# When and in what order the seven right operands of a stage are made, in a one-core fp32 transformer block

## The chip, the cores and the metric

The kernel runs on one NeuronCore of a Trainium2 chip. The metric is the device time of one execution in microseconds (us), from start to end. The profiled execution's span, from its first to its last instruction, is a little shorter than its device time.

## What is computed

The input x has 2048 tokens of 512 features. All of it is float32.

```python
x = x + attn_block(layernorm(x))       # 512x512 matrices Wk, Wv, Wr, Wo, then Wkey/Wval, Wcr
    # inside: kk = mix(h) @ Wkey.T     # 512 -> 2048
    #         kv = silu(kk) @ Wval.T   # 2048 -> 512, gated by sigmoid(... @ Wcr.T)
gate, up = split(layernorm(x) @ w_gate_up.T)   # 512 -> 2 * 2048
x = x + (silu(gate) * up) @ w_down.T           # 2048 -> 512
```

The change touches only the way in which the right-hand operands of two products are prepared: `mix(h) @ Wkey.T` and `layernorm(x) @ w_gate_up.T`.

## The kernel before, in words

Every float32 matrix product is made of three TensorE passes: an operand is split into a high part (a copy rounded to `fp32r`) and a low part (the operand minus its high part), and high x high, high x low and low x high are added in PSUM. In the order of the code, ScalarE makes high parts, VectorE or GpSimd makes low parts by a subtraction.

After the attention part (up to about 250 us of the span) the rest runs as 48 **units**, `unit(u)` on each engine, in **four stages** that begin at units 0, 8, 16 and 32 (`FIRST`). Units 0 to 15 are key units (Wkey), 16 to 47 gate units (w_gate_up). Stages 0 and 1 are the key units of the first and second pair of token blocks; stages 2 and 3 the gate units of the two pairs. A unit takes its left operand from weights (`left`) and its right one from tokens (`combo`). It computes a 2x2 block product by the seven products of a Strassen-Winograd scheme, each of 6 matmuls (`product`, L489 to L499). The right operands of the seven are called B11, T3, T2, B21, T1, T4 and B22, and here each product goes by the name of its right operand. TensorE's order in a unit is: B11, T3, output tiles (slot 0), T2, B21, tiles (slot 1), T1, tiles (slot 2), T4, B22, tiles (slot 3). An output tile is 6 matmuls (L485 to L487) of an earlier unit's result with the down projection; a key unit has two per slot, a gate unit one (unit 17 has tiles in slots 0 and 2 alone).

All units of a stage share one set of right operands. There is one set of places for them, `combo[:, c]`. So at each stage start all seven have to be made anew, each after the last product of the old stage that reads its place (`used[c]`, L366), and before the first product of the new stage that reads it: in the first unit of a stage TensorE waits for `combo_lo` to reach a count which goes by the operand's place in `MADE_ORDER` (L492). Per operand c the steps are

- the sum or difference: `right_sums` (L1211, makes T3 and T1, 4 VectorE operations), `make_t2` (L1241, 2, overwrites B11's tokens), `make_t4` (L1248, 2, overwrites B21's tokens and needs T2);
- `combo_hi_of` (L851): two ScalarE copies of 128x512, after `used[c]`;
- `combo_lo_of` (L1235): two VectorE subtractions of 128x512, each after its copy.

Every engine runs its queue strictly in the order in which the code lists it. Other work in the same queues that the change's order bears on, per unit:

- VectorE: `accumulate` (L1255, frees the PSUM bank of an output tile, which TensorE takes again four tiles later), `seed` (L1308, after T2; TensorE's T1 product waits for it), `sum_v` (L1317, after T1; TensorE's B22 product waits for it, L693), `sums(u + 1)` (L1200, four 128x256 sums for the next unit's left operand in stages 0 and 2), `gate` (L1321, twice in a gate unit; TensorE's T3 product of the next unit waits for both, L679).
- ScalarE: the copies of X (L916, TensorE's T2 waits for it) and of V (L922), `unit_left_hi` (L826, its second part after `sums`), `unit_right_hi`, `key_tile` and `gate_tile` (the SiLUs; TensorE's next unit waits for them).
- GpSimd: `unit_left_lo` (L1477), `unit_right_lo`, `inner_lo_tile`: subtractions of SBUF tiles.

`after` is the new stage in the last unit before it (units 7, 15 and 31). `SUMS_UNIT` names the units in which `right_sums` runs for stages 1, 2 and 3: 4, 14 and 30.

Of the kernel before, what the change touches and what calls it, by code (L numbers as in the profile page):

```python
# [87 lines left out]
A11, A12, A22, S1, S2, S3, S4 = range(SEVEN)  # L88
B11, B21, B22, T4, T1, T2, T3 = range(SEVEN)

MADE_ORDER = (B11, T3, T2, B21, T1, B22, T4)


def stage_of(u):
    return max(n for n in range(STAGE_COUNT) if FIRST[n] <= u)


def stage_start(u):
    return u in FIRST
# [107 lines left out]
def build(nc, x, wts, wide, tall, vectors, identity, out):  # L207
# [3 lines left out]
    with ExitStack() as ctx:  # L211
# [515 lines left out]
        def _(act):  # L727
# [98 lines left out]
            def unit_left_hi(u, part):  # L826

                if part == 0:
                    act.wait_ge(quart_loaded, 16 * (fresh_until(u) + 1))
                    if u >= 2:  # L830
                        act.wait_ge(p3, u - 1)
                    else:
                        act.wait_ge(cr_psum, SUBS * (BLOCKS if u else 2))
                    if u - 2 in FRESH:
                        act.wait_ge(left_kept[u % 2], 16 * same_parity(FRESH, u - 2))
                    act.activation(left[u % 2][:, 0, 0:3, :], quart[:, 1:4, :], ACT.Copy).then_inc(left_hi, 1)
                else:
                    act.wait_ge(sums_done, 4 * (fresh_until(u) + 1))
                    act.activation(left[u % 2][:, 0, 3:7, :], quart[:, 4:8, :], ACT.Copy).then_inc(left_hi, 1)  # L839
# [11 lines left out]
            def combo_hi_of(stage, c):  # L851
                if stage:
                    act.wait_ge(used[c], FIRST[stage])
                else:
                    act.wait_ge(o_psum, SUBS * BLOCKS)
                if c in (T1, T2, T3, T4):
                    act.wait_ge(t_made, 8 * stage + 2 * ((T3, T1, T2, T4).index(c) + 1))
                elif stage == 0:
                    act.wait_ge(ck_made, 2 * KT)
                elif stage == 1:  # L860
                    act.wait_ge(raw_back[0], 16)
                    act.wait_ge(raw_back[1], 16)
                else:
                    act.wait_ge(t3_kept, 2 * SUBS * (stage - 1))
                for k in range(2):
                    act.activation(combo[:, c, k, 0, :], combined(stage, c, k), ACT.Copy).then_inc(combo_hi, 1)
# [6 lines left out]
            def key_tile(u, n, source):  # L873
                tile = 4 * u + n
                b, i = KEY_TILES[n]
                if u:
                    act.wait_ge(inner_lo, tile - RING + 1)
                else:
                    act.wait_ge(op_lo, OPERANDS)
                act.activation(made_at(tile), source[:], ACT.Silu).then_inc(silu_done, 1)  # L880
                if u == 0 and n == 0:
                    act.wait_ge(combo_lo, 2 * SEVEN)
                if u == 1 and n == 0:
                    act.wait_ge(raw_kept[0], 16)
                    act.wait_ge(raw_kept[1], 16)
                act.wait_ge(silu_done, tile + 1)
                inner_hi_tile(tile, 2 * u + b, i)
# [20 lines left out]
            def unit(u):  # L908

                after = stage_of(u + 1) if u + 1 < UNITS and stage_start(u + 1) else None  # L910
                act.wait_ge(p1, u + 1)
                if u:
                    act.wait_ge(silu_done, silu_by(u - 1, 3 if is_key(u - 1) else 1))
                else:
                    act.wait_ge(sr_ready, SUBS * BLOCKS)
                act.activation(Y[:], X[:], ACT.Copy).then_inc(x_copied, 1)  # L916
                if after is not None:
                    combo_hi_of(after, B11)
                act.wait_ge(p7, u + 1)
                if u:  # L920
                    act.wait_ge(v_summed, u)
                act.activation(seventh[:], V[:], ACT.Copy).then_inc(seventh_copied, 1)  # L922
                if u > KEYS:
                    gated_hi(u - 1)
                for j in range(BLOCKS):
                    if u == NORM3_UNIT[j]:
                        norm3(j)
                if stage_start(u) and u:
                    combo_hi_of(stage_of(u), B22)
                if after is not None:  # L930
                    combo_hi_of(after, T3)
                if u + 1 in FRESH:
                    unit_left_hi(u + 1, 0)
                if is_key(u) and u:
                    unit_right_hi(u)
                spread = u in FIRST[1:]
                if u + 1 in FRESH and not spread:
                    unit_left_hi(u + 1, 1)
                act.wait_ge(p2, u + 1)
                if is_key(u):  # L940
                    key_tile(u, 0, X)
                    if u == 0:
                        unit_right_hi(u)
                else:
                    gate_tile(u, 0, X)
                if stage_start(u) and u:
                    combo_hi_of(stage_of(u), T4)
                if not is_key(u):
                    unit_right_hi(u)
                if u + 1 in FRESH and spread:  # L950
                    unit_left_hi(u + 1, 1)
                if after is not None:
                    combo_hi_of(after, T2)
                    combo_hi_of(after, B21)
                    combo_hi_of(after, T1)
                if is_key(u):
                    act.wait_ge(p4, u + 1)
                    key_tile(u, 1, Z)
                    act.wait_ge(v_summed, u + 1)
                    key_tile(u, 2, V)  # L960
                act.wait_ge(p3, u + 1)
                if is_key(u):
                    key_tile(u, 3, Y)
                else:
                    gate_tile(u, 1, Y)
# [49 lines left out]
            unit_left_hi(0, 1)  # L1015
            combo_hi_of(0, B21)
            combo_hi_of(0, T1)
            combo_hi_of(0, B22)
            combo_hi_of(0, T4)
            channel_receptance(3)  # L1020
            act.activation(table[:], minus_half[:, 0, 0:1], ACT.Silu).then_inc(table_loaded, 1)
            for u in range(UNITS):
# [4 lines left out]
        def _(dve):  # L1027
# [207 lines left out]
            def combo_lo_of(stage, c):  # L1235
                for k in range(2):
                    dve.wait_ge(combo_hi, 2 * (SEVEN * stage + MADE_ORDER.index(c)) + k + 1)
                    dve.tensor_tensor(combo[:, c, k, 1, :], combined(stage, c, k), combo[:, c, k, 0, :].bitcast(F32),  # L1238
                                      ALU.subtract).then_inc(combo_lo, 1)
# [91 lines left out]
            def unit(u):  # L1331

                after = stage_of(u + 1) if u + 1 < UNITS and stage_start(u + 1) else None
                def some(slot):
                    for n in tiles_in(u, slot):
                        accumulate(n)

                if stage_start(u) and u:
                    combo_lo_of(stage_of(u), T1)
                some(0)  # L1340
                seed(u)
                if stage_start(u) and u:
                    make_t4(stage_of(u))
                    combo_lo_of(stage_of(u), B22)
                if after is not None:
                    combo_lo_of(after, B11)
                if u + 1 in FRESH and not stage_start(u):
                    sums(u + 1)
                if is_key(u):
                    last_norm(u, 0)  # L1350
                some(1)
                if stage_start(u) and u:
                    combo_lo_of(stage_of(u), T4)
                sum_v(u)
                if u == 0:
                    first_chunk_right_lo()
                if stage_start(u) and u and u + 1 in FRESH:
                    sums(u + 1)
                if after is not None:
                    make_t2(after)  # L1360
                    combo_lo_of(after, T3)
                some(2)
                if not is_key(u):
                    gate(u, 0)
                    gate(u, 1)
                if after is not None:
                    combo_lo_of(after, T2)
                some(3)
                if u in SUMS_UNIT:
                    right_sums(SUMS_UNIT.index(u))  # L1370
                last_norm(u, 1)
                if after is not None:
                    combo_lo_of(after, B21)

            first_norm1()
            last_of_r_lo()
# [53 lines left out]
            combo_lo_of(0, B21)  # L1430
            make_t4(0)
            combo_lo_of(0, T1)
            combo_lo_of(0, B22)
            combo_lo_of(0, T4)
            sums(1)
            for u in range(UNITS):
                unit(u)
# [175 lines left out]
```

## Time and profile before

| what | value |
|---|---|
| device time, median of 3 runs | 1074.23 us (1073.85 to 1074.23) |
| device time of the profiled execution | 1074.51 us |
| its span | 1072.7 us |
| TensorE busy | 1057.1 us, 99% |
| VectorE, ScalarE, GpSimd busy | 59%, 45%, 50% |
| granted TensorE clock, mean | 0.998 |

Engines in rows: PE is TensorE's matmul, DVE is VectorE, ACT is ScalarE, POOL is GpSimd. In a row of a timeline stand the start (us from the span's start), the time it took, the engine, the line, the operation, the tiles written and read, the shapes and the number of instructions merged into the row; a bracket tells how long the engine was idle before it and what released it. A matmul's recorded 0.39 us overlaps the next one's, so idle time on TensorE is read from starts: here and below a "group" is six matmuls, those of one product or one output tile.

### The profile page before, as it was taken

To read this page: it belongs to the slowest core of one execution; us is meant where nothing else is said; L and a number is where in the kernel's file an instruction comes from. 1 tells how busy PE (TensorE), PEld (TensorE's weight loads), DVE (VectorE), ACT (ScalarE), POOL (GpSimd) and SP (SyncE) were. 2 spreads that over 40 slices of the span, in tenths; PEclk is the share of its full clock that TensorE was granted. 3 is DMA by queue.
4 is the path that set the end of the run, shared out by engine and by line. 5 is a ranking of instruction groups with operands and counts; after the bars stand their busy time and mean duration, and the time that the engine had idled before them with its cause. 6 is when DMAs were issued, how large, how long until landed. Compare 5 with 4: busy or idle time off the path is not lost.

```text
span 1072.7 us, 13182 instructions
## 1 busy us (share of the span) xinstructions
PE 1057.1 (99%) x4748; PEld 873.8 (81%) x4748; DVE 632.5 (59%) x1104; ACT 484.2 (45%) x808; POOL 540.2 (50%) x453
## 2 busy tenths in 40 slices
PE   7999999999999999999999999999999999999998
PEld 6888888788888888888887888888887888888887
DVE  7888656786545545555459567676658333333334
ACT  6866676766444454333355433434354222222221
POOL 6686373735755545445345655555553333333322
PEclk9999999999999999999999999999999999999999
DMA  8002042267653345742412757564554464344422
GB/s 317 1 1 40 1 99 83 95 202 282 231 182 122 128 157 158 225 128 89 157 50 99 243 208 238 207 188 153 197 183 150 149 234 155 106 141 152 153 79 79
DMA packets 45234, 157.19 MB, mean 147 GB/s; under 512 B 4080, under 2 KB 4208, under 8 KB 40560
## 3 DMA queue, kind: packets, MB, share of 16 engines
q1 hardware_dynamic: 29712, 108.02, 28.8%
q0 software_dynamic: 15168, 48.24, 15.0%
q8 instruction: 38, 0.62, 0.2%
q14 instruction: 28, 0.23, 0.1%
q10 hardware_dynamic: 288, 0.09, 0.0%
HBM read 97.60 MB, written 58.72 MB: 146 GB/s over the span
## 4 chain that ended last, share of the span: by engine, by line
PE 87%; DVE 7%; POOL 2%; ACT 1%; DMA 1%; issue 1%; SPq 0%; ACTq 0%; DVEq 0%
PE bank L485 15%; PE bank L486 15%; PE bank L487 15%; PE bank L496 13%; PE bank L497 13%; PE bank L498 13%; DVE combo L1238 2%; DMA quart<-wide 1%; POOL operand L1459 1%; PE bank L555 1%; PE bank L653 1%; DVE resid L1264 1%; POOL weights L1447 0%; POOL weights L1459 0%; DVE raw L1245 0%
## 5 line engine op out<-in xcount | busy, mean ns | idle before, releaser
L1264 DVE TENSOR_TENSOR resid<-bank,resid 128x512 f32<-128x512 f32 x240 | 165.1, 690 | 239.8 <-PE bank L487 238.5
L1503 POOL TENSOR_TENSOR inner<-made,inner 128x512 fp32r<-128x512 f32 x128 | 166.8, 1326 | 200.5 <-ACT inner L871 200.5
L496 PE MATMUL bank<-combo,left 128*128 128x512 f32 x672 | 262.7, 391 | 4.7 <-DVE combo L1238 3.1
L498 PE MATMUL bank<-combo,left 128*128 128x512 f32 x672 | 261.5, 389 | 0.0
L497 PE MATMUL bank<-combo,left 128*128 128x512 f32 x672 | 261.5, 389 | 0.0
L485 PE MATMUL bank<-right,inner 128*128 128x512 f32 x512 | 199.2, 389 | 0.0
L486 PE MATMUL bank<-right,inner 128*128 128x512 f32 x512 | 199.2, 389 | 0.0
L487 PE MATMUL bank<-right,inner 128*128 128x512 f32 x512 | 199.2, 389 | 0.0
L1481 POOL TENSOR_TENSOR left<-quart,left 128x512 fp32r<-128x512 f32 x96 | 115.4, 1225 | 91.3 <-ACT left L839 46.8
L496 PEld LDWEIGHTS bank<-combo,left 128*128 128x128 f32 x672 | 126.1, 188 | 34.1 <-DVE combo L1238 4.0
L498 PEld LDWEIGHTS bank<-combo,left 128*128 128x128 f32 x672 | 126.1, 188 | 26.2
L497 PEld LDWEIGHTS bank<-combo,left 128*128 128x128 f32 x672 | 126.2, 188 | 25.7
L485 PEld LDWEIGHTS bank<-right,inner 128*128 128x128 f32 x512 | 96.1, 188 | 20.1
L487 PEld LDWEIGHTS bank<-right,inner 128*128 128x128 f32 x512 | 96.1, 188 | 20.0
L486 PEld LDWEIGHTS bank<-right,inner 128*128 128x128 f32 x512 | 96.1, 188 | 19.9
L1498 POOL TENSOR_TENSOR right<-tall_staged,right 128x512 fp32r<-128x512 f32 x62 | 80.8, 1312 | 59.2 <-ACT right L849 59.2
L892 ACT ACTIVATE made<-bank 128x512 f32<-128x512 f32 x64 | 38.1, 595 | 154.0 <-PE bank L498 154.0
L1459 POOL TENSOR_TENSOR operand<-made,operand 128x512 fp32r<-128x512 f32 x64 | 83.6, 1406 | 35.1 <-ACT operand L736 35.1
L1329 DVE TENSOR_TENSOR made<-bank,made 128x512 f32<-128x512 f32 x64 | 44.2, 691 | 60.4 <-ACT made L892 39.1
L871 ACT ACTIVATE inner<-made 128x512 fp32r<-128x512 f32 x128 | 77.2, 628 | 2.5 <-DVE made L1329 0.2
L880 ACT ACTIVATE made<-bank 128x512 f32<-128x512 f32 x64 | 37.6, 587 | 85.7 <-PE bank L498 85.7
L485 PE MATMUL bank<-operand,weights 128*128 128x512 f32 x176 | 69.5, 395 | 1.8 <-ACT held L763 1.8
(133 smaller groups left out, 1457.7 us busy)
## 6 DMA issues: line engine op xcount, KB each, us to landing
kept_left<-left SPq DMA_DIRECT2D x24, 1792.0 KB, 8.1
left<-kept_left POOLq DMA_DIRECT2D x24, 1024.0 KB, 6.9
left<-kept_left POOLq DMA_DIRECT2D x24, 768.0 KB, 5.0
tall_staged<-tall SPq DMA_DIRECT2D x64, 256.0 KB, 2.9
quart<-wide SPq DMA_DIRECT2D x24, 512.0 KB, 4.2
raw<-kept SPq DMA_DIRECT2D x32, 256.0 KB, 6.3
landed<-wts SPq DMA_DIRECT2D x20, 256.0 KB, 6.3
resid<-x POOLq DMA_DIRECT2D x4, 1024.0 KB, 9.2
```

Of the source, the lines that this page charges most:

```text
L485: pe.matmul(acc, left(0), right(0), start=first, stop=False)
L486: pe.matmul(acc, left(0), right(1), start=False, stop=False)
L487: return pe.matmul(acc, left(1), right(0), start=False, stop=last)
L496: pe.matmul(acc[:], hi, combo[:, c, k, 0, :], start=fresh and k == 0, stop=False, skip_group_check=True)
L497: pe.matmul(acc[:], hi, combo[:, c, k, 1, :], start=False, stop=False, skip_group_check=True)
L498: mm = pe.matmul(acc[:], lo, combo[:, c, k, 0, :], start=False, stop=k == 1, skip_group_check=True)
L871: act.activation(inner[:, h % 4, i, 0, :], made_at(n), ACT.Copy).then_inc(inner_hi, 1)
L1264: dve.tensor_tensor(tile, A[s][:], tile, ALU.add).then_inc(added, 1)
L1459: pool.tensor_tensor(place(kind, b, k, 1), made[:, (n + k) % RING, :], place(kind, b, k, 0).bitcast(F32), ALU.subtract).then_inc(op_lo, 1)
L1481: lo = pool.tensor_tensor(left[u % 2][:, 1, a[0]:a[0] + n, :], quart[:, a[0] + 1:a[0] + 1 + n, :], left[u % 2][:, 0, a[0]:a[0] + n, :].bit ...
L1498: pool.tensor_tensor(right[:, g % 2, i, 1, :], tall_staged[i][:], right[:, g % 2, i, 0, :].bitcast(F32), ALU.subtract).then_inc(right_lo, 1)
L1503: pool.tensor_tensor(inner[:, h % 4, i, 1, :], made_at(n), inner[:, h % 4, i, 0, :].bitcast(F32), ALU.subtract).then_inc(inner_lo, 1)
```

## The change

Three things, by the diff:

- In the last unit of a stage (7, 15, 31) ScalarE copies T2 just before that unit's first SiLU, and T4 before the last one, where T4 was copied in the first unit of the new stage. VectorE makes B11's low part first of all, T2 (`make_t2`) before `seed`, T3's low part behind `seed`, T2's low part before `sum_v`, B21's low part and T4 (`make_t4`) before the tiles of slot 2, and T1's low part before the tiles of slot 3. In the first unit of the stage T4's and B22's low parts are left.
- `right_sums` stands in units 4, 14 and 30 behind `sum_v`, no more behind the tiles of slot 3.
- T4 and B22 change places in `MADE_ORDER`, in ScalarE's and VectorE's queues ahead of unit 0, and in the first unit of a stage. TensorE's own order is unchanged.

No operation is added or taken away.

```diff
@@ -88,7 +88,7 @@
 A11, A12, A22, S1, S2, S3, S4 = range(SEVEN)
 B11, B21, B22, T4, T1, T2, T3 = range(SEVEN)
 
-MADE_ORDER = (B11, T3, T2, B21, T1, B22, T4)
+MADE_ORDER = (B11, T3, T2, B21, T1, T4, B22)
 
 
 def stage_of(u):
@@ -936,6 +936,8 @@
                 spread = u in FIRST[1:]
                 if u + 1 in FRESH and not spread:
                     unit_left_hi(u + 1, 1)
+                if after is not None:
+                    combo_hi_of(after, T2)
                 act.wait_ge(p2, u + 1)
                 if is_key(u):
                     key_tile(u, 0, X)
@@ -943,14 +945,11 @@
                         unit_right_hi(u)
                 else:
                     gate_tile(u, 0, X)
-                if stage_start(u) and u:
-                    combo_hi_of(stage_of(u), T4)
                 if not is_key(u):
                     unit_right_hi(u)
                 if u + 1 in FRESH and spread:
                     unit_left_hi(u + 1, 1)
                 if after is not None:
-                    combo_hi_of(after, T2)
                     combo_hi_of(after, B21)
                     combo_hi_of(after, T1)
                 if is_key(u):
@@ -958,6 +957,8 @@
                     key_tile(u, 1, Z)
                     act.wait_ge(v_summed, u + 1)
                     key_tile(u, 2, V)
+                if after is not None:
+                    combo_hi_of(after, T4)
                 act.wait_ge(p3, u + 1)
                 if is_key(u):
                     key_tile(u, 3, Y)
@@ -1015,8 +1016,8 @@
             unit_left_hi(0, 1)
             combo_hi_of(0, B21)
             combo_hi_of(0, T1)
+            combo_hi_of(0, T4)
             combo_hi_of(0, B22)
-            combo_hi_of(0, T4)
             channel_receptance(3)
             act.activation(table[:], minus_half[:, 0, 0:1], ACT.Silu).then_inc(table_loaded, 1)
             for u in range(UNITS):
@@ -1335,42 +1336,43 @@
                     for n in tiles_in(u, slot):
                         accumulate(n)
 
-                if stage_start(u) and u:
-                    combo_lo_of(stage_of(u), T1)
-                some(0)
-                seed(u)
-                if stage_start(u) and u:
-                    make_t4(stage_of(u))
-                    combo_lo_of(stage_of(u), B22)
                 if after is not None:
                     combo_lo_of(after, B11)
+                some(0)
+                if after is not None:
+                    make_t2(after)
+                seed(u)
+                if after is not None:
+                    combo_lo_of(after, T3)
+                if stage_start(u) and u:
+                    combo_lo_of(stage_of(u), T4)
                 if u + 1 in FRESH and not stage_start(u):
                     sums(u + 1)
                 if is_key(u):
                     last_norm(u, 0)
                 some(1)
                 if stage_start(u) and u:
-                    combo_lo_of(stage_of(u), T4)
+                    combo_lo_of(stage_of(u), B22)
+                if after is not None:
+                    combo_lo_of(after, T2)
                 sum_v(u)
                 if u == 0:
                     first_chunk_right_lo()
                 if stage_start(u) and u and u + 1 in FRESH:
                     sums(u + 1)
+                if u in SUMS_UNIT:
+                    right_sums(SUMS_UNIT.index(u))
                 if after is not None:
-                    make_t2(after)
-                    combo_lo_of(after, T3)
+                    combo_lo_of(after, B21)
+                    make_t4(after)
                 some(2)
                 if not is_key(u):
                     gate(u, 0)
                     gate(u, 1)
                 if after is not None:
-                    combo_lo_of(after, T2)
+                    combo_lo_of(after, T1)
                 some(3)
-                if u in SUMS_UNIT:
-                    right_sums(SUMS_UNIT.index(u))
                 last_norm(u, 1)
-                if after is not None:
-                    combo_lo_of(after, B21)
 
             first_norm1()
             last_of_r_lo()
@@ -1430,8 +1432,8 @@
             combo_lo_of(0, B21)
             make_t4(0)
             combo_lo_of(0, T1)
+            combo_lo_of(0, T4)
             combo_lo_of(0, B22)
-            combo_lo_of(0, T4)
             sums(1)
             for u in range(UNITS):
                 unit(u)
```

## Rows read from the trace of the kernel before

**Rows 1.** The page, engines: busy us, share of the span, instructions.
```profile
PE 1057.1 (99%) x4748; PEld 873.8 (81%) x4748; DVE 632.5 (59%) x1104; ACT 484.2 (45%) x808; POOL 540.2 (50%) x453
```
**Rows 2.** Waits of PE: who for whom, us in total, times, longest.
```profile
PE bank L496 <- DVE combo L1238: 3.1, 2, 2.0
```
**Rows 3.** Timeline of PE at the starts of stages 2 and 3.
```profile
571.91 0.47 PE L496 MATMUL bank<-combo,left 128*128 128x512 f32 x1 [0.33 <-issue]
...
579.71 0.50 PE L496 MATMUL bank<-combo,left 128*128 128x512 f32 x1 [0.75 <-DVE bank L1315]
...
583.91 0.50 PE L496 MATMUL bank<-combo,left 128*128 128x512 f32 x1 [1.19 <-DVE combo L1238]
...
589.69 0.50 PE L496 MATMUL bank<-combo,left 128*128 128x512 f32 x1
...
824.60 0.39 PE L486 MATMUL bank<-right,inner 128*128 128x512 f32 x1
824.83 0.39 PE L487 MATMUL bank<-right,inner 128*128 128x512 f32 x1
827.17 0.50 PE L496 MATMUL bank<-combo,left 128*128 128x512 f32 x1 [1.95 <-DVE combo L1238]
```
**Rows 4.** Timelines of DVE and POOL: the same operations together and apart.
```profile
563.85 3.00 DVE L1245 TENSOR_TENSOR raw<-raw 128x512 f32<-128x512 f32 x2
...
563.30 2.99 POOL L1481 TENSOR_TENSOR left<-quart,left 128x512 fp32r<-128x512 f32 x2 [3.19 <-ACT left L839]
...
809.51 1.29 DVE L1245 TENSOR_TENSOR raw<-raw 128x512 f32<-128x512 f32 x2
...
587.09 2.54 POOL L1481 TENSOR_TENSOR left<-quart,left 128x512 fp32r<-128x512 f32 x2 [8.04 <-ACT left L839]
...
572.68 5.78 DVE L1238 TENSOR_TENSOR combo<-raw,combo 128x512 fp32r<-128x512 f32 x4
```
**Rows 5.** Timelines of PE, DVE and POOL in unit 30 and early in 31.
```profile
792.38 0.39 PE L496 MATMUL bank<-combo,left 128*128 128x512 f32 x1
...
793.94 0.70 DVE L1319 TENSOR_TENSOR bank<-bank,e 128x512 f32<-128x512 f32 x1 [0.67 <-PE bank L498]
...
798.65 0.69 DVE L1329 TENSOR_TENSOR made<-bank,made 128x512 f32<-128x512 f32 x1 [1.23 <-ACT made L892]
...
799.99 1.29 DVE L1223 TENSOR_TENSOR extra<-raw 128x512 f32<-128x512 f32 x2
...
792.71 4.50 POOL L1481 TENSOR_TENSOR left<-quart,left 128x512 fp32r<-128x512 f32 x4 [3.62 <-ACT left L836]
797.16 1.29 POOL L1498 TENSOR_TENSOR right<-tall_staged,right 128x512 fp32r<-128x512 f32 x1
...
800.54 0.39 PE L496 MATMUL bank<-combo,left 128*128 128x512 f32 x1
```
**Rows 6.** Timelines of DVE, ACT, POOL and PE in unit 15.
```profile
555.19 1.98 POOL L1481 TENSOR_TENSOR left<-quart,left 128x512 fp32r<-128x512 f32 x2 [4.28 <-ACT left L836]
557.13 2.98 POOL L1498 TENSOR_TENSOR right<-tall_staged,right 128x512 fp32r<-128x512 f32 x2
...
561.71 0.42 DVE L1209 TENSOR_TENSOR quart<-quart 128x256 f32<-128x256 f32 x1
...
563.25 0.69 DVE L1319 TENSOR_TENSOR bank<-bank,e 128x512 f32<-128x512 f32 x1
...
562.16 1.06 ACT L839 ACTIVATE left<-quart 128x1024 fp32r<-128x1024 f32 x1 [6.01 <-DVE quart L1209]
...
565.98 0.39 PE L496 MATMUL bank<-combo,left 128*128 128x512 f32 x1
```
**Rows 7.** Timelines of ACT and PE ahead of unit 0 and in it.
```profile
247.51 1.15 ACT L866 ACTIVATE combo<-held 128x512 fp32r<-128x512 f32 x2 [2.65 <-DVE held L1252]
248.57 1.55 ACT L824 ACTIVATE raw<-bank 128x512 f32<-128x512 f32 x3
...
250.95 1.28 ACT L1021 ACT_TABLE_LOAD   x1
...
252.99 0.50 PE L496 MATMUL bank<-combo,left 128*128 128x512 f32 x1
...
276.70 0.50 PE L496 MATMUL bank<-combo,left 128*128 128x512 f32 x1 [0.25 <-DVE bank L1319]
```

## The prediction, made before the change was run

> **What bounds the kernel now.** I read the page's busy shares first: TensorE is busy 99% of the span [rows 1], so nothing elsewhere can pay unless it removes a hole on TensorE. The list of TensorE's waits then says what the holes are: the largest item in the units is the low parts of the right operands, two waits, 3.1 us in all [rows 2]. That list counts from a matmul's modelled end, so I took sizes from the start-to-start times of TensorE's timeline [rows 3]. In a full stretch a matmul starts 0.227 us after the one before (824.60 to 824.83 [rows 3]), so a group of six takes 1.36 us. Counting groups against the starts there gives these holes. Start of stage 2: T3 of unit 16 at 571.91 instead of 571.42 (0.49), T1 at 579.71 instead of 578.80 (0.91), T4 at 583.91 instead of 582.57 (1.34), T3 of unit 17 at 589.69 instead of 589.48 (0.21). Start of stage 3: T4 of unit 32 at 827.17 instead of 825.06 (2.11). A product after a hole also runs about 0.1 longer (0.50 for 0.39 in its first row). Together **3.37 us at unit 16/17 and 2.25 at unit 32**. The start of stage 1 has no hole. So 5.6 us, 0.5%, is all that the change can win.
>
> **The port that two engines share.** One fact of the trace sizes everything below. `make_t2`, VectorE's pair of subtractions with both inputs in SBUF, takes 1.29 us alone and 3.00 when GpSimd subtracts at the same time; GpSimd's own pair goes from 2.54 to 2.99 [rows 4]. The two take turns: with GpSimd's queue full, such a VectorE operation ends 0.55 after the GpSimd operation it waited for, GpSimd's next one is held 0.45, and the next VectorE operation ends 1.74 after the last. Four in a row took 5.78 [rows 4], where alone they take 0.60 each. VectorE operations that read PSUM are not touched (0.70 at 793.94 while GpSimd runs from 792.71 [rows 5]).
>
> The Trainium skill, page "SBUF — State Buffer", section "SBUF: two separate sides", goes further: the pair is an exclusive lock held for the whole instruction and the loser fully blocks. By that sentence a turn would cost GpSimd the full VectorE time (0.68) and not the 0.45 that the rows show; it is priced as a rival below.
>
> **Part 1: the swap ahead of unit 0.** Before, ScalarE copied B22 while it waited for T4's sum, copied T4 at 247.51, then three sigmoids at 248.57, a fourth, the table load at 250.95, and the copy of X for which T2's product waits (252.99) [rows 7]. Now B22's copy stands behind T4's, 1.04 us of pitch. The fourth sigmoid started only at 250.34, when TensorE gave it its tile, 0.3 after ScalarE was free, so 0.72 us of it arrives at the table load and at T2's product: **+0.72**. Bounds: 0.3, if the hole at 276.70 (0.41 [rows 7]) takes up the difference, since it hangs on a transfer; 1.04, if no slack counts.
>
> **Part 2: stage 1 (units 4, 7, 8).** Key units have eight output tiles to hide under and no gates; unit 8's left operand comes by a transfer, so GpSimd has no `unit_left_lo` in unit 7. In a walk like the ones below the tightest wait (`seed` before T1) keeps 1.4 us. **0**, bounds 0 and 0.3.
>
> **Part 3: `right_sums` in unit 14.** Four subtractions of 0.60, one turn lost; the tiles of slot 2 are accumulated some 2 us later, and their banks are wanted two slots later. **0.**
>
> **Part 4: unit 15, stage 2.** Walk of the new order, from the times of the old one [rows 6] and the turns above. VectorE: B11 low before the tiles come; `make_t2` arrives at 555.9, GpSimd is busy from 555.19 to 560.1, both halves wait a turn, end 558.1; `seed` 558.7 (TensorE's T1 needs it at 560.54, covered); T3 low, two turns behind `unit_right_lo`, ends 561.5; the four `sums` end 563.0, where they ended 562.13. ScalarE: second part of `unit_left_hi` (562.16 before) 563.0 to 564.1, and only behind it, in the same queue, T2's copies, to 565.1. VectorE's T2 low waits for those and stands ahead of `sum_v`. GpSimd starts its `unit_left_lo` pair the moment ScalarE's part is there, at 564.2, so T2 low loses two turns: 566.0 and 567.7. `sum_v` ends 568.3, where it ended 563.9. B22's product was due at 565.98 and waits for it: **a new hole of 2.37 + 0.1**. Queued behind it on VectorE: B21 low, T4, the tiles of slot 2. T4's sum loses two more turns (571.7, 573.4), ScalarE's T4 copy ends 574.6, the last SiLU and the copy of X follow to 576.25; T2's product of unit 16 is due 576.62: covered by 0.37 only. T1, T4, B22 of unit 16 are then there in time: those holes go. `sums(17)` ends 585.4 instead of 585.9, and from it hang ScalarE 1.1 and GpSimd 2.5, so T3 of unit 17 starts 589.17, still 0.3 + 0.1 late. Come 2.9, go 3.37: **-0.5**. Bounds: nothing comes but the last 0.4 (-3.0), one more turn lost (+1.2).
>
> **Part 5: units 30 to 32, stage 3.** `sum_v` of unit 30 starts 793.94, 1.56 after T1's group starts [rows 5]; `right_sums` now arrives at 794.57. It ran free at 799.99. GpSimd has four `unit_left_lo` operations in 792.71 to 797.21 and one of `unit_right_lo` to 798.45 [rows 5], so each of the four VectorE operations waits a turn: 795.3, 797.0, 798.7, 800.4. Behind them stand a tile and the two `gate`s, 0.6 each: the second gate ends 802.17, where it ended 799.35. TensorE's T3 of unit 31 was due at 800.54 and waits for that gate: **new hole, 1.68 + 0.1**. From there, with TensorE shifted: `make_t2` loses two turns to `inner_lo_tile`, `seed` ends 809.23 against T1 due 809.13 (0.15 + 0.1); T2 low loses one turn to `unit_right_lo`, `sum_v` ends 813.9 against B22 due 813.47 (0.43 + 0.1); B21 low, T4's sum, its copy, the last SiLU and the gate end 818.65 against T3 of unit 32 due 818.09 (0.61 + 0.1). Sum 3.3. The old hole of 2.25 goes: **+1.06**. Bounds: without the first hole -0.7; one more turn lost +2.8.
>
> **Sum.** +0.72 + 0 + 0 - 0.5 + 1.06 = +1.3 us. The profiled execution took 1074.51 (span 1072.7 and 1.8 around it), so its like would take 1075.8; it stood 0.28 over the median, so against the median of 1074.23 I say **1075.5**.
>
> **Rivals.**
> (a) *The waits are hidden and the holes just go.* It needs VectorE to win its turns: for it, every new wait is under 2.5 us; against it, GpSimd is loaded by the very ScalarE copies that precede. 5.6 less 0.4 kept in unit 17, plus 0.7: 1069.7. Chance 0.12.
> (b) *`right_sums` passes ahead of GpSimd in unit 30.* GpSimd's operations are queued back to back, so who gets the port at a change is read from four cases only [rows 4]. Then the 1.79 hole is absent: 1073.7. Chance 0.15.
> (c) *Slower: T4's copy becomes the gate of the stage.* It stands in ScalarE ahead of the last SiLU, which the next unit's V and X copies follow. Covered by 0.37 in unit 16 and by nothing in 32; if the sum for T4 meets one GpSimd operation more than I count, 1.7 comes at each boundary, 1.35 and 1.7: 1078.5. It decides as soon as VectorE reaches T4 more than 0.4 us later than in my walk. Chance 0.15.
> (d) *The port is held for the whole of VectorE's instruction.* 0.23 more per turn, four turns before T3 of unit 31 and six before B22 of unit 15, some 2.1 us: 1077.6. This is what the page "SBUF — State Buffer" of the Trainium skill says. The pair together and apart speaks against it [rows 4] (GpSimd's pair grew by 0.45, not by 0.68). Chance 0.03.
> (e) The change does less than it says: T2 in unit 15 still comes after the next unit's left operand. That is in the sum already.
>
> **How the numbers follow.** Forecast 0.55, (a) 0.12, (b) 0.15, (c) 0.15, (d) 0.03. A measurement here can tell about 0.2% (2.15 us) from no change, so "same" is 1072.1 to 1076.4. The forecast's own spread is about 1 us either way, 0.1 of its 0.55 above 1076.4 and 0.01 below 1072.1. Same: 0.44 + 0.15 = 0.59, slower: 0.10 + 0.15 + 0.03 = 0.28, faster: 0.12 + 0.01 = 0.13. The range goes from 1072.4, which leaves out (a), to 1078.0, which leaves out half of (c).
>
> **What would show it.** Right: no hole at T1 and T4 of unit 16 and at T4 of unit 32; instead B22 of unit 15 late by about 2.4 behind `sum_v`, T3 of unit 31 late by about 1.7 behind the second `gate`, T3 of unit 32 late by about 0.6; `right_sums` of unit 30 stretched from 2.5 to 5.8 us; T2's product of unit 0 later by 0.7; stage 1 whole. Wrong: `sum_v` of unit 15 before 566, or `right_sums` of unit 30 in under 4 us.

## The result, and the profile after

| | before | after |
|---|---|---|
| device time, median of 10 runs | 1074.23 us | 1077.26 us (1076.15 to 1078.12) |
| ratio to before | | 1.0024, 95% interval 1.0015 to 1.0033 |
| profiled execution: device time, span | 1074.51, 1072.7 us | 1077.5, 1075.7 us |

The kernel became 0.24% slower, 3.0 us. The interval lies clear of 1, and 1077.26 lies 0.9 us above 1076.4, where the prediction had drawn the line between "same" and "slower". One of the 11 executions of "right sums late" below took 2171.88 us, twice all the others, and stands in no ratio; nothing here shows why. The page after has the same instructions on each engine [rows 1]:

```profile
span 1075.7 us, 13182 instructions
...
PE 1058.8 (98%) x4748; PEld 874.9 (81%) x4748; DVE 640.4 (60%) x1104; ACT 484.4 (45%) x808; POOL 542.9 (50%) x453
```

VectorE's busy time rose from 632.5 to 640.4 us with the same 1104 operations, so the 8 us lie inside them; the timelines of the first experiment show where. The list of TensorE's waits in the units (who for whom, us in total, times, longest) names other causes than before, when the largest item was the low parts [rows 2]:

```profile
PE bank L496 <- DVE bank L1320: 3.0, 3, 2.3
PE bank L496 <- DVE made L1330: 1.6, 1, 1.6
PE bank L496 <- issue: 0.6, 1, 0.6
PE bank L496 <- ACT bank L916: 0.4, 1, 0.4
```

L1320 is `sum_v`, L1330 the gate, L916 the copy of X (VectorE's lines after are one further on than before). In TensorE's timeline these are the first matmuls of T2 in unit 0, B22 in unit 15, T3 and B22 in unit 31 and T3 in unit 32; the last row is T4 of unit 32, at which the kernel before had its longest hole [rows 3] and which now follows without one:

```profile
253.67 0.50 PE L496 MATMUL bank<-combo,left 128*128 128x512 f32 x1 [0.41 <-ACT bank L916]
...
569.25 0.50 PE L496 MATMUL bank<-combo,left 128*128 128x512 f32 x1 [2.25 <-DVE bank L1320]
...
803.83 0.47 PE L496 MATMUL bank<-combo,left 128*128 128x512 f32 x1 [1.59 <-DVE made L1330]
...
815.62 0.50 PE L496 MATMUL bank<-combo,left 128*128 128x512 f32 x1 [0.32 <-DVE bank L1320]
...
820.64 0.47 PE L496 MATMUL bank<-combo,left 128*128 128x512 f32 x1 [0.64 <-issue]
...
830.26 0.39 PE L496 MATMUL bank<-combo,left 128*128 128x512 f32 x1
```

So every hole of before at T1 and T4 is gone. Of the new ones three stand in the last unit of a stage (B22 of unit 15, T3 and B22 of unit 31), where before had none. Behind the one at 569.25 something else follows. The same timeline 0.8 us later:

```profile
570.04 0.40 PE L496 MATMUL bank<-combo,left 128*128 128x512 f32 x1
570.28 0.56 PE L497 MATMUL bank<-combo,left 128*128 128x512 f32 x1
570.64 0.63 PE L498 MATMUL bank<-combo,left 128*128 128x512 f32 x1
571.07 0.63 PE L485 MATMUL bank<-right,inner 128*128 128x512 f32 x1
...
573.20 0.63 PE L487 MATMUL bank<-right,inner 128*128 128x512 f32 x1
573.63 0.46 PE L485 MATMUL bank<-right,inner 128*128 128x512 f32 x1
573.92 0.40 PE L486 MATMUL bank<-right,inner 128*128 128x512 f32 x1
```

From 570.3 to 573.7 matmuls start 0.427 us apart instead of 0.227. The busy time of that stretch (its length, the engines in the page's order, then granted clock, DMA share and GB/s) shows the clock at half, 1.2 GHz:

```profile
570.40:573.60 3.20, 3.20 (x9) 2.46 (x8) 3.17 (x3) 1.11 (x2) 3.13 (x2) 0.50 1.03 422
```

To compare kernels free of what lies before the units, I take the time from the start of one unit's B11 product to another's. One table serves all that follows. A hole is counted from one matmul's start to the next one's, beyond 0.227 us; the wait in a row's bracket counts from a modelled end and is some 0.16 us shorter.

| kernel | units 0 to 4, us | 15 to 18, us | 30 to 34, us | ratio to before, 95% interval |
|---|---|---|---|---|
| before | 71.57 | 51.09 | 63.89 | |
| after | 72.30 | 51.76 | 65.31 | 1.0024 (1.0015 to 1.0033) |
| right sums late | 72.56 | 51.78 | 63.67 | 1.0006 (0.9997 to 1.0015) |
| sum_v first | 72.26 | 50.10 | 64.80 | 1.0001 (0.9992 to 1.0010) |
| and T4's copy late | 72.25 | 49.15 | 64.14 | 0.9986 (0.9977 to 0.9995) |
| port kept free | 72.15 | 49.64 | 63.63 | 0.9987 (0.9978 to 0.9996) |
| unit 0's order back | 71.71 | 50.67 | 65.33 | 1.0004 (0.9995 to 1.0013) |
| swap alone | 71.92 | 51.87 | 64.04 | 1.0007 (0.9998 to 1.0016) |
| all hidden | 71.87 | 48.78 | 62.52 | 0.9956 (0.9943 to 0.9970) |
| gates first | 71.84 | 48.78 | 62.17 | 0.9958 (0.9946 to 0.9971) |
| all hidden, sum_v behind T2 | 72.12 | 50.22 | 63.06 | 0.9987 (0.9978 to 0.9996) |
| all hidden, unit 30's sums early | 71.58 | 48.79 | 64.15 | 0.9974 (0.9963 to 0.9984) |

Between units 4 and 15 and between 18 and 30 before and after agree within 0.02 us. One ratio point of 0.001 is 1.07 us.

### The profile page after: what moved, and what is told of

Read it like the earlier page. It is cut to its first block, busy times and chain, and to the rows that moved or that the text cites. A ratio compares the mean times of both kernels' runs of the same rounds, so it can differ in the third digit from the quotient of the medians.

```text
span 1075.7 us, 13182 instructions
## 1 busy us (share of the span) xinstructions
PE 1058.8 (98%) x4748; PEld 874.9 (81%) x4748; DVE 640.4 (60%) x1104; ACT 484.4 (45%) x808; POOL 542.9 (50%) x453
## 4 chain that ended last, share of the span: by engine, by line
PE 87%; DVE 6%; ACT 2%; POOL 2%; issue 2%; DMA 1%; SPq 0%; DVEq 0%; ACTq 0%
PE bank L485 15%; PE bank L487 15%; PE bank L486 15%; PE bank L496 13%; PE bank L498 13%; PE bank L497 13%; DMA quart<-wide 1%; DVE combo L1239 1%; POOL operand L1461 1%; PE bank L555 1%; PE bank L653 1%; POOL weights L1449 0%; DVE raw L1246 0%; POOL weights L1461 0%; ACT combo L866 0%
## 5 line engine op out<-in xcount | busy, mean ns | idle before, releaser
L1330 DVE TENSOR_TENSOR made<-bank,made 128x512 f32<-128x512 f32 x64 | 44.1, 691 | 57.3 <-ACT made L892 37.4
```

## The experiments

### The shared port, tested by keeping GpSimd away

```diff
 # gpsimd, unit(u), ahead of unit_left_lo(u + 1, 1)
+                if u == FIRST[2] - 1:
+                    pool.wait_ge(combo_lo, 2 * (2 * SEVEN + 3))
+                if u == FIRST[3] - 2:
+                    pool.wait_ge(t_made, 8 * 3 + 4)
```

> The changed kernel with two waits added on GpSimd and VectorE's order untouched: in unit 30 its second pair for the next left operand starts only when right_sums is done, in unit 15 only when T2's low part is done. Theory (VectorE is late because it takes turns with GpSimd at the port): right_sums of unit 30 takes 2.5 to 3.2 us instead of 5.8 and the hole at T3 of unit 31 is gone; in unit 15 T2's low part takes 1.3 us instead of 3.05, sum_v ends 1.7 us sooner, and the hole at B22 falls from 2.4 to about 0.6; part of that comes back at T2 of unit 16 behind T4's copy (1 to 1.5); time 1073 to 1074.5. Rival (VectorE's own length or its inputs set these times): the subtractions stay as long, holes as before, time 1077 or more.

Median 1073.51 us; by the ratios about 4 us less than after. VectorE's timeline of unit 30, first after, then with the port kept free (L1224 and L1227 are `right_sums`):

```profile
795.48 0.70 DVE L1320 TENSOR_TENSOR bank<-bank,e 128x512 f32<-128x512 f32 x1 [0.67 <-PE bank L498]
796.09 2.41 DVE L1224 TENSOR_TENSOR extra<-raw 128x512 f32<-128x512 f32 x2
798.41 3.47 DVE L1227 TENSOR_TENSOR raw<-raw,raw 128x512 f32<-128x512 f32 x2
801.82 0.68 DVE L1265 TENSOR_TENSOR resid<-bank,resid 128x512 f32<-128x512 f32 x1
802.42 1.27 DVE L1330 TENSOR_TENSOR made<-bank,made 128x512 f32<-128x512 f32 x2
```

```profile
792.53 0.70 DVE L1320 TENSOR_TENSOR bank<-bank,e 128x512 f32<-128x512 f32 x1 [0.67 <-PE bank L498]
793.14 1.31 DVE L1224 TENSOR_TENSOR extra<-raw 128x512 f32<-128x512 f32 x2
794.37 1.28 DVE L1227 TENSOR_TENSOR raw<-raw,raw 128x512 f32<-128x512 f32 x2
795.58 0.68 DVE L1265 TENSOR_TENSOR resid<-bank,resid 128x512 f32<-128x512 f32 x1
```

The same four operations at the same place take 5.8 us with GpSimd in the port and 2.5 without. The hole at T3 of unit 31 is gone. In unit 15, T2's low part and `sum_v`, first after, then with the port kept free:

```profile
565.53 3.05 DVE L1239 TENSOR_TENSOR combo<-raw,combo 128x512 fp32r<-128x512 f32 x2 [0.45 <-ACT combo L866]
568.51 0.68 DVE L1320 TENSOR_TENSOR bank<-bank,e 128x512 f32<-128x512 f32 x1
```

```profile
564.70 1.29 DVE L1239 TENSOR_TENSOR combo<-raw,combo 128x512 fp32r<-128x512 f32 x2 [0.45 <-ACT combo L866]
565.91 0.69 DVE L1320 TENSOR_TENSOR bank<-bank,e 128x512 f32<-128x512 f32 x1
```

The hole at B22 of unit 15 is 0.66 instead of 2.42. Some comes back at T2 of unit 16 behind the copy of X, less than expected: 0.73, and 0.14 at an output tile ahead of it, where I had said 1 to 1.5. The theory of turns holds; VectorE's own length is not the cause.

### right_sums back behind slot 3

```diff
                 if stage_start(u) and u and u + 1 in FRESH:
                     sums(u + 1)
-                if u in SUMS_UNIT:
-                    right_sums(SUMS_UNIT.index(u))
...
                 some(3)
+                if u in SUMS_UNIT:
+                    right_sums(SUMS_UNIT.index(u))
                 last_norm(u, 1)
```

> The changed kernel with one part undone: right_sums stands behind the tiles of slot 3 again, in units 4, 14 and 30. Theory (the late T3 product of unit 31 is right_sums losing its turns at the shared port ahead of the two gates): the hole of 1.75 us at T3 of unit 31 is gone, the holes at B22 of units 15 and 31 and at T3 of unit 32 stay within 0.3 us, the time falls by 1.7 to 1.9 us, to about 1075.5. Rival (VectorE just has too much to do ahead of the stage, wherever the sums stand): the hole comes back at T1 or B22 of unit 31 and the time falls by less than 0.7 us.

Median 1075.56. The 1.76 us hole at T3 of unit 31 is gone. T1 of unit 31 is 0.40 late instead of 0.16, B22 of unit 31 and T3 of unit 32 as late as after (0.49, 0.81), and B22 of unit 15 too (2.41). Units 30 to 34 are 1.64 us shorter. The rival would have had all of it come back; 0.24 did.

### sum_v ahead of T2's low part, and then T4's copy late

```diff
 # x2: vector, unit(u)
+                sum_v(u)
                 if after is not None:
                     combo_lo_of(after, T2)
-                sum_v(u)
```

> The changed kernel with one exchange in the last unit of a stage: VectorE takes sum_v before T2's low part. Theory 1 (the hole at B22 of unit 15 hides a second one: T4's copy on ScalarE ahead of the last SiLU and of the copy of X): the 2.4 us hole at B22 of unit 15 goes, a hole of 1.8 to 2.4 us comes at T2 of unit 16, and at T3 of unit 32 what B22 of unit 31 gave (0.5 us) comes back; time 1076 to 1077.5. Rival (the holes are separate terms): both B22 holes go with the slow matmuls behind the one of unit 15, 2.9 + 1.6 us, to 1072.8.

```diff
 # x3: as x2, and scalar, unit(u)
                 if stage_start(u) and u:
+                    combo_hi_of(stage_of(u), T4)
                     combo_hi_of(stage_of(u), B22)
...
-                if after is not None:
-                    combo_hi_of(after, T4)
                 act.wait_ge(p3, u + 1)
```

> As sum_v first, and T4's copy on ScalarE stands in the first unit of the stage behind the copy of V, ahead of B22's. Theory 1 (T4's copy gates the stage): no hole of over 0.3 us in units 15 to 17, the granted clock is whole there, the 1.75 us hole at T3 of unit 31 stays, T3 of unit 32 keeps about 0.6 us; time about 1072.5 (1071.8 to 1073.3). Rival (the port turns on VectorE make T4 itself late): T4 of unit 16 or 32 waits again by over 1 us, time 1074 or more.

Medians 1074.84 and 1073.42. With sum_v first the hole at B22 of unit 15 is gone and 2.17 us come back, as much as expected but at two places: 1.43 at an output tile and 0.74 at T2 of unit 16. Even so the time missed my 1076 to 1077.5, for two reasons. The clock held, so units 15 to 18 are 1.66 us shorter than after. And of the 0.5 at B22 of unit 31 only 0.12 came back at T3 of unit 32 (0.80 after, 0.92 here). TensorE's waits from 540 to 620 us, with sum_v first:

```profile
PE bank L485 <- DVE resid L1265: 1.3, 1, 1.3
PE bank L496 <- ACT bank L916: 0.6, 1, 0.6
```

and with T4's copy late as well:

```profile
PE bank L485 <- DVE resid L1264: 1.3, 1, 1.3
```

The copy of X was a gate, as the theory said: its wait goes when T4's copy goes, and T3 of unit 32 falls from 0.92 late to 0.25, where I had expected 0.6 to stay. The other gate I had not named: the tiles of slot 2 are accumulated behind B21's low part and T4's sum, and the output tile of unit 16 waits for the bank of the first of them. My walk set no time for it. With the changed kernel's order and the clock held (the profiled execution with unit 0's order back, below) that bank came free 1.3 us before TensorE took it; with TensorE 2.4 us further on it is late. That is why T4's copy late came out 0.1 us above its range: 1.43 where at most 0.3 was expected. The rival "separate terms" for sum_v first is refuted at unit 16, where 2.17 of 2.42 came back; at unit 32 it is nearer to the truth than my theory, since 0.35 of 0.47 stayed away. The rival for T4's copy late is refuted: T4 itself was in time.

### The order ahead of unit 0 put back

```diff
+FIRST_ORDER = (B11, T3, T2, B21, T1, B22, T4)   # for stage 0 alone
...
-            combo_hi_of(0, T4)
             combo_hi_of(0, B22)
+            combo_hi_of(0, T4)
 # and the two low parts in the same order
```

> The changed kernel with the order ahead of unit 0 put back (B22 copied before T4, for that stage alone). Theory (B22's copy no longer fits into ScalarE's wait for T4's sum and pushes the fourth sigmoid, the table load and the copy of X): T2 of unit 0 starts 0.7 us sooner, the quart transfer that unit 1's B22 product hangs on 0.1 to 0.2 more, everything else stays; the time falls by 0.6 to 0.9 us, to about 1076.4. Rival (the hole at B22 of unit 1 hangs on the transfer alone and eats it): under 0.4 us.

Median 1075.67, units 0 to 4 0.59 us shorter and the 0.14 at B11 of unit 0 gone too: 0.73, in the expected band. B22 of unit 1 is 0.54 late where it was 0.62 after and 0.41 before [rows 7]: it hangs on its transfer and follows, it does not absorb. The median fell by more, 1.6 us, and in the profiled execution the rest is in units 15 to 18. The hole at B22 of unit 15 has the same size, and the clock behind it held. (A mean granted clock of 0.997, which the two profiled executions with two stretches at half have, stands in 1 of 11 executions here and in 5 of 10 of after.) Its wait, and the stretch from 1.0 us behind it on, in the columns of the stretch at half clock above:

```profile
567.57 0.50 PE L502 MATMUL bank<-combo,left 128*128 128x512 f32 x1 [2.25 <-DVE bank L1326]
...
568.60:571.80 3.20, 3.20 (x15) 2.63 (x14) 3.17 (x3) 1.24 (x3) 3.00 (x2) 1.00 1.08 405
```

### The swap alone, on the kernel before

```diff
-MADE_ORDER = (B11, T3, T2, B21, T1, B22, T4)
+MADE_ORDER = (B11, T3, T2, B21, T1, T4, B22)
+FIRST_ORDER = (B11, T3, T2, B21, T1, B22, T4)   # for stage 0 alone
 # scalar, unit(u), in the first unit of a stage
-                    combo_hi_of(stage_of(u), B22)      # behind the copy of V
                     combo_hi_of(stage_of(u), T4)
+                    combo_hi_of(stage_of(u), B22)
 # vector, unit(u)
                     make_t4(stage_of(u))
-                    combo_lo_of(stage_of(u), B22)
+                    combo_lo_of(stage_of(u), T4)
                 some(1)
-                    combo_lo_of(stage_of(u), T4)
+                    combo_lo_of(stage_of(u), B22)
                 sum_v(u)
```

> The kernel before with one part of the change alone: in stages 1 to 3 T4's copy and low part stand ahead of B22's in the first unit, all else as before (ahead of unit 0 too). Theory (T4's product waits for two low parts of B22 that it does not need, one of them behind a turn at the port): the hole at T4 of unit 32 falls from 2.11 to under 0.3 us and that of unit 16 from 1.35 to under 0.3, T3 and T1 of unit 16 keep 0.49 and 0.91; B22 of unit 16 or 32 at most 0.5 late; 2.7 to 3.5 us faster than before. Rival (what B22 gives up it takes back one product later, since VectorE has the same work): under 1.5 us faster.

Median 1075.72: no gain; my theory falls and the rival stands. T4 of unit 32 is 0.08 late instead of 2.11, but B22, the next product, is 2.00 late:

```profile
829.04 0.51 PE L502 MATMUL bank<-combo,left 128*128 128x512 f32 x1 [1.83 <-DVE bank L1324]
```

L1324 is `sum_v`, which stands behind B22's low part. VectorE's timeline there:

```profile
824.20 1.29 DVE L1243 TENSOR_TENSOR combo<-raw,combo 128x512 fp32r<-128x512 f32 x2 [0.76 <-ACT combo L872]
825.41 0.68 DVE L1269 TENSOR_TENSOR resid<-bank,resid 128x512 f32<-128x512 f32 x1
826.01 2.37 DVE L1243 TENSOR_TENSOR combo<-raw,combo 128x512 fp32r<-128x512 f32 x2
828.30 0.69 DVE L1324 TENSOR_TENSOR bank<-bank,e 128x512 f32<-128x512 f32 x1
```

The same operations in another order, with the same lost turn (2.37 us for two): only the product that waits is another. In unit 16 it is the same (T4 0.38, B22 0.89), and T3 of unit 17 is 0.91 late where it was 0.20: units 15 to 18 take 0.8 us more than before. So the swap, one of the three parts of the change, wins nothing by itself.

### All hidden, and the two bad moves put back into it alone

"All hidden" is the changed kernel with the four repairs above: right_sums late, sum_v first, T4's copy late, unit 0's order back, and

```diff
+                some(2)
                 if after is not None:
                     combo_lo_of(after, B21)
                     make_t4(after)
-                some(2)
```

> The T4-copy-late kernel with right_sums behind slot 3 again, the order ahead of unit 0 put back, and the tiles of slot 2 accumulated ahead of B21's low part and T4's sum in the last unit of a stage. Theory (the gates in turn were sum_v, right_sums ahead of the gates, T4's copy ahead of the copy of X, and, as the runs before showed, the accumulation behind T4's sum, 1.43 us at the output tile of unit 16): no hole over 0.5 us after unit 1; 4.5 to 5.2 us faster than the kernel before. Rival (a fifth gate appears when these go): a new hole of over 1 us in units 15 to 17 or 31 to 33, under 3.5 us faster.

Median of 5 executions 1070.52, by the ratio 0.44% less than before (0.30% to 0.57%), 4.7 us. TensorE's waits from 240 us on:

```profile
PE bank L502 <- POOL left L1488: 0.6, 1, 0.6
PE bank L502 <- DVE bank L1325: 0.6, 1, 0.6
PE bank L502 <- DVE bank L1321: 0.2, 1, 0.2
```

The first is T3 of unit 17, 0.81 late behind `unit_left_lo`, over the 0.5 that I had allowed; the second is B22 of unit 1 with its transfer. Making the operands in the last unit does hide them, when what TensorE waits for comes first in each queue.

> As all hidden, and the two gates of unit 31 stand ahead of B21's low part and T4's sum as well. Theory: T3 of unit 32 (0.25 us late in the T4-copy-late kernel) starts in time; VectorE waits some 1.5 us for the last SiLU, T4 has 2 us of cover or more: 0 to 0.4 us faster than all hidden. Rival (that wait makes T1's or T4's low part late): a hole at T1 or T4 of unit 32 of over 0.5 us, slower than all hidden.

Here `gate` stands ahead of B21's low part and T4's sum too. Median 1070.77. T3 of unit 32 is in time (0.24 late in all hidden) and units 30 to 34 are 0.35 us shorter; the whole executions overlap those of all hidden, so that the gain shows in the trace and not in the time.

Back in alone, `sum_v` behind T2's low part:

> The all-hidden kernel (1070.5 us) with one move of the change put back alone: in the last unit of a stage sum_v stands behind T2's low part. Theory: the hole at B22 of unit 15 is 2.4 us again and that at B22 of unit 31 0.5, while what VectorE is late with anyway (0.81 at T3 of unit 17, 0.25 at T3 of unit 32) is swallowed: 1.6 to 2.1 us slower than all hidden where the clock holds, about 1.6 more where it falls behind the hole; median 1072.1 to 1074. Rival (sum_v's place alone costs nothing, the hole in the changed kernel needed the T4 copy too): within 0.5 us of all hidden.

Median 1073.16. B22 of unit 15 is 2.41 late again, B22 of unit 31 0.50, and T3 of unit 17 (0.81) is swallowed. Units 15 to 18 and 30 to 34 take 1.44 + 0.54 = 1.98 us more, as expected. The medians differ by 2.6; where the other 0.6 lies is not shown (a mean granted clock of 1.000 stood in 3 of 5 executions of all hidden and in 1 of 11 here, and the clock is treated below). The place of `sum_v` is enough for the hole. Unit 30's right_sums early, alone:

> The all-hidden kernel with one move of the change put back alone: right_sums for stage 3 stands ahead of the tiles and gates of unit 30. Theory: the hole at T3 of unit 31 is back at 1.75 us, the 0.40 at T1 of unit 31 shrinks to about 0.16, the rest stays: 1.3 to 1.8 us slower than all hidden, about 1072.1. Rival (in the changed kernel the late gates were only one of several waits that ended together): under 0.7 us slower.

Median 1072.47 (8 executions). T3 of unit 31 is 1.75 late again, T1 of unit 31 0.15; units 30 to 34 take 1.63 us more, and the median 1.95. Both rivals are refuted: each move costs by itself what the walk gave it.

## Why the prediction was right in its mechanisms and short in its size

I forecast 1075.5 with "same" as the likeliest; the time is 1077.26, inside the range and 0.9 us beyond the bound of "same". The number alone would have spoken for rival (d) and its 1077.6; the places of the holes speak against it. By parts, profiled execution against profiled execution (+3.0 where I had +1.3):

- **Ahead of unit 0: right, 0.15 short.** 0.72 forecast for T2's product, 0.70 measured: 0.14 at B11 of unit 0, which waits for the first of the delayed sigmoids, and 0.56 behind it. Another 0.17 comes later, so units 0 to 4 show 0.73. The case of the lower bound, that the hole at unit 1 takes up the delay, did not come: that hole grew from 0.41 to 0.62, since its transfer was issued 0.5 later, behind VectorE work that moved too, and took 0.4 longer.
- **Stage 1 and right_sums in unit 14: right.** No hole, nothing between units 4 and 15.
- **Unit 15: right to 0.05 us.** B22 2.37 forecast, 2.42 measured, behind `sum_v`, behind T2's low part in 3.05 us (two turns lost), behind ScalarE's copies, behind the next unit's left operand.
- **Units 16 to 18: the term that I left out.** Forecast -0.5. Where the clock held, in the profiled execution of the kernel with unit 0's order back, units 15 to 18 show -0.42. In the profiled execution of after it is +0.67, since the 2.25 us wait was followed by 3.4 us at half clock. Nine matmul intervals, 0.06 to 0.20 us longer each, add up to 1.6; the 0.33 at T3 of unit 17 was swallowed. The row for this was in the trace of before, near 28 us, where the clock also halves behind a wait of TensorE for an operand; I read the mean of 0.998 and did not ask what made it:

```profile
27.07 0.50 PE L485 MATMUL bank<-operand,weights 128*128 128x512 f32 x1 [1.82 <-ACT held L763]
...
28.20:31.60 3.40, 3.40 (x10) 2.62 (x9) 3.37 (x11) 2.37 (x5) 3.40 (x3) 0.50 0.00 0
```

- **Units 30 to 32: right in place, 0.36 short.** 1.06 forecast, 1.42 measured. T3 of unit 31 1.75 (1.68 forecast), T1 0.16 (0.15), B22 0.47 (0.43), T3 of unit 32 0.80 (0.61). Ahead of the last stand T4's sum, its copy, the last SiLU and the gate; my walk gave a time for the gate alone, so which of them was mis-sized stays open.
- **Sum without the clock:** 0.87 - 0.42 + 1.42 = 1.9 us. Two executions of after with a mean granted clock of 1.000 took 1076.15 and 1076.33 us, 2.5 over the 14 such executions of before that were timed beside the experiments (median 1073.78); the 0.6 between the two figures is not accounted for.

Of the rivals, (a), that the waits hide, is what the same operations do in another order (all hidden), not in this one. (b), that right_sums passes ahead of GpSimd, did not occur in any profiled execution. (c) named a gate that is real: the copy of X behind T4's copy is 0.74 late as soon as B22's hole is gone, but in the changed kernel it was covered, as the walk said. At unit 32, where the walk had no cover for it, T4's copy makes 0.67 of the 0.92 at T3 (sum_v first against T4's copy late). (d), by which GpSimd would be held for the whole VectorE instruction, is refuted: by that reading of the Trainium skill, page "SBUF — State Buffer", section "SBUF: two separate sides", B22 of unit 15 would have been 1.4 us later than the walk (six turns of 0.23), and it came 0.05 later; T3 of unit 31 would have been 0.9 later and came 0.07 later.

## What to carry to other kernels

Moving work earlier on an in-order engine moves everything queued behind it later: list, for the new order, which wait of the busy engine each passed operation feeds, and put those first. Two engines that take turns at one port price an operation by what the other has queued at that moment, so the same four subtractions cost 2.5 or 5.8 us by their place alone. And one long wait of TensorE can cost more than itself: the one of 2.25 us here cost 1.6 us more in some executions, while those of 1.6 us did not in any that was profiled.

## What the runs showed of the hardware

- **Strict turns.** With both queues full, VectorE (two SBUF inputs) and GpSimd alternated in every stretch looked at, never two in a row for either: VectorE's operations ended some 1.7 us apart where alone they start 0.6 apart. One operation to a row, in unit 30 of after:

```profile
796.19 1.75 POOL L1483 TENSOR_TENSOR left<-quart,left 128x512 fp32r<-128x512 f32 x1
796.72 1.78 DVE L1224 TENSOR_TENSOR extra<-raw 128x512 f32<-128x512 f32 x1
797.90 1.74 POOL L1483 TENSOR_TENSOR left<-quart,left 128x512 fp32r<-128x512 f32 x1
798.41 1.77 DVE L1227 TENSOR_TENSOR raw<-raw,raw 128x512 f32<-128x512 f32 x1
```

VectorE's operations with a PSUM input took 0.69 beside GpSimd and alone.
- **The clock behind a wait.** TensorE's wait of 2.25 us before B22 of unit 15 was followed by 3.4 us at half the granted clock in the profiled execution of after and in that of right sums late, and by none in those of unit 0's order back and of sum_v behind T2, with the same wait. Near 27 us every kernel has a wait of 1.8 to 2.1 us; in 5 of the 12 profiled executions half clock followed, in 7 it did not, among them three of the four with 2.08 us or more. The waits of 1.95 and 1.83 us in unit 32 (before, swap alone) and those of 1.6 us at T3 of unit 31 (five kernels) were followed by none. The two profiled executions with two stretches at half have a mean granted clock of 0.997. Over all executions 0.997 stood in 5 of 10 of after and 5 of 33 of the three other kernels with the 2.25 us wait, in 2 of 11 of swap alone, in 1 of the 72 of before that were timed beside the experiments, and in none of the 51 of the other six kernels. What decides it in one execution and not in another stays open.
- **The first matmul after a wait** has the next one start 0.30 to 0.34 us later instead of 0.23, so each hole costs about 0.1 more than its length.
